# Attention seams: transposed keys and queries in banks of their own, the first head one slot ahead

## The chip, the cores and the metric

The kernel runs on one core of one Trainium2 chip. Its five engines are PE (TensorE, matmuls and transposes), DVE (VectorE), ACT (ScalarE), POOL (GpSimd) and SP (SyncE, which here only issues DMAs). PE writes into PSUM, which has eight banks of 128 partitions x 512 floats; DVE and ACT read them. The metric is the device time of one execution in microseconds (us), the median of several.

## The reference, cut to what matters

The input is `x` (4 x 512 x 512) with a context of the same shape, both float32. Two residual blocks follow each other:

```python
x = x + quantised_matmul(layernorm(x), ctx)          # both sides rounded to fp8 in blocks of 128
h = rmsnorm(layernorm(x), attn_norm_w)
q, k, v = h @ q_w.T, h @ k_w.T, h @ v_w.T            # 16 query heads, 4 key/value heads, 128 wide
q, k = rope(rmsnorm(q)), rope(rmsnorm(k))
attn = softmax(causal(q @ k.T / sqrt(128))) @ v      # four query heads share one key head
hidden = layernorm(x) + attn @ o_w.T
h2 = rmsnorm(hidden, ffn_norm_w)
out = x + hidden + sum over the top 2 of 8 experts of weight * down(silu(gate(h2)) * up(h2))
```

Queries, keys and values must be exact to float32 beyond what one pass of a matmul gives. So the kernel splits an operand into a high part (`_hi`, a copy rounded by ACT) and a low part (`_lo`, source minus high part, by DVE) and adds three products: high x high, high x low, low x high.

## The kernel before, in words

The program has a start, 16 iterations of attention (`for it in range(NIT)`) and the experts. An iteration `it = 4 b + g` is one batch `b` and one key head `g`. It has four heads `h`, and each head has four rows of 128 queries (`q = 0..3`), whose scores, maxima, exponentials and sums are made by PE (`score`, lines 696 to 705), DVE (`maxima`, L1264; `invert`, L1270 and, for the last row, the scaling L1275) and ACT (`exponentials`, L944). The probabilities of the head two heads back (`LAG = 2`) are turned by PE (`transpose_p`, L713), copied by ACT (`copy_p`, L950) and multiplied with the values (`values`, L724); the result is split by ACT (`hi_attn`, L958) and DVE (`lo_attn`, L1281).

Between these stand pieces of other work, put into slots by tables. A slot is `(head, place)` with place 1 to 3, and `units` yields for each slot, in this order, the pieces of the tables `FRONT_FIRST`, `ROUTE_FIRST`, `FILL`, `FRONT`, `ROUTE`, the weight splits and the experts' weights (`ew`). All engines walk the same slots, each doing its share, in the fixed order of its own program; semaphores tie the engines together. Place 1 of PE lies behind the scores of rows 0 and 1, place 2 behind row 2's score and ahead of the value products and row 3's score, place 3 at the end of the head. On ACT place 2 stands behind the copies of the probabilities and ahead of the last row's exponential. On DVE place 2 stands behind the last row's maximum and ahead of its reciprocal and scaling, place 3 behind `lo_attn`.

The pieces that matter here:

- `q`, `kv`: projections of the next iteration (`project`, L669), into banks 0 and 1; POOL ends them with a rope addition (L504).
- `o`: the output projection of the iteration before (`output`, L741), into banks 0 and 1 in turn, added to the hidden state by DVE (`add_output`, L1291). `m`: DVE scales the keys (`apply_norms`, L1258).
- `t` and `u`: the keys (piece 0) and the queries of heads 0 to 3 (pieces 1 to 4) are turned: four 128 x 128 transposes on PE (`transpose_qk`, L693), the high part by ACT (`hi_qk`, L963), the low part by DVE (`lo_qk`, L1286). Pieces 0 to 3 stand in the last slot (3,3), piece 4 (`u`) in the slot (0,1) of the next iteration. Their banks are `TR = (5, 6, 2, 5, 2)`. Piece 3 uses the bank of piece 0 and waits for its subtraction; piece 4 uses that of piece 2.
- `x..`, `y..`, `h..`: the next batch's first block, spread over the iterations g = 0 to 2. `xp` is its product with the context (L587, bank 2, added by DVE at L1140). `ht` turns the rows of the attention input (L613, bank 2; high part L869, low part L1166); the last of the four rows is in `FRONT_FIRST` at (3,3) of g = 2, ahead of piece 0.
- `rl`: the router's logits of the batch before (L647, bank 2, read by DVE at L1205), at g = 3; the last at (3,3).
- `ew`: in ten slots of an iteration from iteration 5 on, a piece of an expert's weights is split (L899 on ACT, L1193 or L1191 on DVE) and stored by DMA; ACT waits for the store before it reuses its buffer.

The first score of a head waits until the low part of its queries is there; before the first head's turned probabilities go to banks 5 and 6, PE waits for all of pieces 0 to 3:

```python
if i >= 2:
    need(pe, qk_lo, (G + 1) * j + {2: 0, 3: 1, 4: 3}[i])
...
pe.wait_ge(qk_lo, (G + 1) * it + h + 2)      # score, row 0 of head h
...
pe.wait_ge(qk_lo, (G + 1) * it + G)          # ahead of transpose_p
```

The end of an iteration together with the begin of the next is called a seam below; there are 15, numbered by the iteration that ends. At seams 2, 6 and 10 the slot (3,3) holds `ht` 3, at seams 7 and 11 `rl` 3, and at seams 1, 5 and 9 the slot (3,2) holds `xp` 2.

Of the kernel before, what the change touches and what calls it, by code (L numbers as in the profile page):

```python
# [19 lines left out]
B, S, D = 4, 512, 512  # L20
P = 128
NT = B * S // P
TT = S // P
# [3 lines left out]
G = HQ // HKV  # L27
# [42 lines left out]
def build(nc, x, ctxT, w_attn, wqkvo, qn, kn, cos, sin, w_ffn, gate, wexp, ident_d, mask_d, dispf_d, disph_d, out):  # L70
    with ExitStack() as ctx:
# [13 lines left out]
        def load_expert(sp, e, down):  # L85
# [22 lines left out]
        (2, 2): (('kv', 3),),  # L108
        (2, 3): (('o', 0), ('n', 0), ('o', 1)),
        (3, 1): (('m', 0), ('o', 2)),  # L110
        (3, 2): (('o', 3),),
        (3, 3): (('t', 0), ('t', 1), ('t', 2), ('t', 3))}


FRONT = ({(0, 1): (('cm', 0), ('cs', 0)),
# [23 lines left out]
          (1, 2): (('yh', 0), ('yh', 1)),  # L139
          (2, 1): (('yr', 0), ('yh', 2), ('yh', 3), ('ht', 0)),  # L140
          (2, 3): (('ht', 1),),
          (3, 1): (('ht', 2),)},
         {})
FRONT_FIRST = ({}, {}, {(3, 3): [("ht", 3)]}, {})
ROUTE = {(0, 1): (('rs', 0), ('rs', 1)),
         (1, 1): (('rs', 2),),
         (1, 2): (('rs', 3), ('rn', 0), ('rt', 0)),
# [26 lines left out]
NRAW = len(RAW)  # L174
RING_A = 6
LAG = 2


def need(engine, sem, count):

    if count > 0:
        engine.wait_ge(sem, count)


def units(it, h, place):


    b, g = divmod(it, HKV)
    slot = (h, place)
    if b + 1 < B:  # L190
        yield from FRONT_FIRST[g].get(slot, ())
    if g == HKV - 1 and b:
        yield from ROUTE_FIRST.get(slot, ())
    for kind, i in FILL.get(slot, ()):
        if (kind != "o" or it) and (it + 1 < NIT or kind in "ou"):
            yield kind, i
    if b + 1 < B:
        yield from FRONT[g].get(slot, ())
    if g == HKV - 1 and b:
        yield from ROUTE.get(slot, ())  # L200
    if it + 2 < HKV:
        yield from SPLIT_Q.get(slot, ())
    if 1 <= it <= HKV:
        yield from SPLIT_O.get(slot, ())
    if it >= FIRST_E and slot in SPLIT_E:
        m = (it - FIRST_E) * len(SPLIT_E) + SPLIT_E.index(slot)
        if m < NPIECE:
            yield "ew", m


def mixer(nc, x, ctxT, w_attn, wqkvo, wexp, wx_dram, qn, kn, cos, sin, w_ffn, gate_d, ident_d, mask_d, ident, logits, wcolf, extra, last_acc,
# [3 lines left out]
    with ExitStack() as ctx:  # L215
# [28 lines left out]
        kT = [[sb(f"kT{i}_{n}", [P, S], F32R) for n in ("hi", "lo")] for i in range(2)]  # L244
        v = [sb(f"v{i}", [P, TT, HD]) for i in range(LAG + 1)]
        prob = [sb(f"prob{i}", [P, sum(KEYS)]) for i in range(LAG + 1)]
        pT = sb("pT", [P, sum(QS)])
# [26 lines left out]
        zero = tables_at[:, 7 * HD:7 * HD + H]  # L274
        bank = [ctx.enter_context(nc.psum_tensor(f"bank{i}", [P, S], F32)) for i in range(8)]
        AUX, SC, PT, PV = 2, 3, 5, 7
        TR = (PT, PT + 1, AUX, PT, AUX)
        FIRST_T, FIRST_P = (PT, PT + 1, AUX, PV), (0, 1, SC, SC + 1)

        const_in, table_in, table_step = sem("const_in"), sem("table_in"), sem("table_step")  # L280
# [8 lines left out]
        q_rotated, kv_rotated, rope_added, k_ready = sem("q_rotated"), sem("kv_rotated"), sem("rope_added"), sem("k_ready")  # L289
        qk_tr, qk_hi, qk_lo = sem("qk_tr"), sem("qk_hi"), sem("qk_lo")  # L290
# [3 lines left out]
        at_hi, at_lo, o_done, o_added = sem("at_hi"), sem("at_lo"), sem("o_done"), sem("o_added")  # L294
# [12 lines left out]
        cm_turned, cm_row, cm_spread, cm_back, first_added = (sem(n) for n in ("cm_turned", "cm_row", "cm_spread", "cm_back", "first_added"))  # L307
# [262 lines left out]
        def _(pe):  # L570
# [79 lines left out]
            def project(j, t, kv):  # L650
                b = j // HKV
                if j == 0:
                    pe.wait_ge(hlo_ready, t + 1)
                elif t == 0 and not kv:
                    pe.wait_ge(hlo_ready, TT * (b + 1))
                if t == 0 and j < HKV:
                    pe.wait_ge(wqkv_lo, QKV * j + (QKV if kv else KC))
                elif t == 0:
                    for i in range(2):
                        pe.wait_ge(wkv_in[i] if kv else wq_in[i], 16 * (j - HKV + 1))  # L660
                need(pe, kv_rotated if kv else q_rotated, TT * j + t if j else t - 1)
                if t == 0:
                    need(pe, o_added, TT * (j - 2))
                if j == 0 and not kv:
                    pe.wait_ge(x1_ready, TT)
                o = kv_bank(j, t)[:, 0:2 * HD] if kv else q_bank(j, t)[:, :]
                for k in range(KC):
                    for n, (a, c) in enumerate(SPLITS):
                        last = nc.tensor.matmul(o, hT[a][:, k, t * P:(t + 1) * P], wkv(j, c, k) if kv else wq(j, c, k),  # L669
                                                start=(k == 0 and n == 0), stop=(k == KC - 1 and n == 2))  # L670
                last.then_inc(projkv if kv else projq, 1)

            def transpose_qk(j, i):
                it = j - 1
                if i == 1 and j == 0:
                    pe.wait_ge(first_added, TT)
                if i == 0:
                    pe.wait_ge(k_ready, j + 1)
                    need(pe, pt_copied, 16 * it + 4 * (G - LAG))
                if i == 2 and j:  # L680

                    b, g = divmod(it, HKV)
                    if g == 1 and b + 1 < B:
                        pe.wait_ge(x1_ready, TT * (b + 1) + 3)
                    if g == 2 and b + 1 < B:
                        pe.wait_ge(hlo_ready, TT * (b + 2))
                    if g == HKV - 1 and b:
                        pe.wait_ge(lg_ready, TT * b)
                if i >= 2:
                    need(pe, qk_lo, (G + 1) * j + {2: 0, 3: 1, 4: 3}[i])  # L690
                at = G * HD if i == 0 else (i - 1) * HD
                for t in range(TT):
                    last = nc.tensor.transpose(bank[TR[i]][:, t * P:(t + 1) * P], r[:, t, at:at + HD], ident[:, :])  # L693
                last.then_inc(qk_tr, 1)
# [12 lines left out]
            def transpose_p(s, j):  # L707
# [4 lines left out]
                for q in range(j, TT):  # L712
                    last = nc.tensor.transpose(bank[PT + j % 2][:, (q - j) * P:(q - j + 1) * P],  # L713
                                               prob[s % (LAG + 1)][:, P_AT[q] + j * P:P_AT[q] + (j + 1) * P], ident[:, :])
                last.then_inc(pt_tr, 1)
# [37 lines left out]
                project(0, t, False)  # L753
            for t in range(TT):
                project(0, t, True)
            for i in range(G):
                transpose_qk(0, i)
            for it in range(NIT):
                b, g = divmod(it, HKV)
                work = {"q": lambda t: project(it + 1, t, False), "kv": lambda t: project(it + 1, t, True), "o": lambda t: output(it - 1, t),  # L760
                        "t": lambda i: transpose_qk(it + 1, i), "u": lambda i: transpose_qk(it, i),
                        "xt": lambda t: transposes_x(b + 1, t), "xp": lambda t: product_x(b + 1, t), "ht": lambda t: transposes_h(b + 1, t),
                        "rt": lambda t: transposes_r(b - 1, t), "rl": lambda t: route(b - 1, t)}

                def fill(h, place):
                    for kind, i in units(it, h, place):
                        if kind in work:
                            work[kind](i)

                for h in range(G):  # L770
                    s = G * it + h - LAG
                    score(it, h, 0)
                    score(it, h, 1)
                    fill(h, 1)
                    if h == 0 or s == 0:

                        pe.wait_ge(qk_lo, (G + 1) * it + G)
                    if s >= 0:
                        transpose_p(s, 0)
                        transpose_p(s, 1)  # L780
                    score(it, h, 2)
                    fill(h, 2)
                    if s >= 0:
                        values(s, 0)
                        transpose_p(s, 2)
                        values(s, 1)
                        transpose_p(s, 3)
                    score(it, h, 3)
                    if s >= 0:
                        values(s, 2)  # L790
                        values(s, 3)
                    fill(h, 3)
# [20 lines left out]
        def _(act):  # L813
# [144 lines left out]
                nc.scalar.activation(aT[0][:, s % RING_A, :], bank[PV][:, :], ACT.Copy).then_inc(at_hi, 1)  # L958

            def hi_qk(j, i):  # L960
                act.wait_ge(qk_tr, (G + 1) * j + i + 1)
                o = kT[j % 2][0][:, :] if i == 0 else qT[0][:, i - 1, :]
                nc.scalar.activation(o, bank[TR[i]][:, :], ACT.Copy).then_inc(qk_hi, 1)  # L963

# [34 lines left out]
                square_kv(0, t)  # L999
            hi_qkv(1, 4)  # L1000
            hi_qkv(1, 5)
            for i in range(G):
                hi_qk(0, i)
            for it in range(NIT):
                b, g = divmod(it, HKV)
# [44 lines left out]
        def _(dve):  # L1050
# [230 lines left out]
                nc.vector.tensor_tensor(aT[1][:, s % RING_A, :], bank[PV][:, :], aT[0][:, s % RING_A, :].bitcast(F32), ALU.subtract).then_inc(at_lo, 1)  # L1281

            def lo_qk(j, i):
                dve.wait_ge(qk_hi, (G + 1) * j + i + 1)
                hi, lo = (kT[j % 2][0][:, :], kT[j % 2][1][:, :]) if i == 0 else (qT[0][:, i - 1, :], qT[1][:, i - 1, :])
                nc.vector.tensor_tensor(lo, bank[TR[i]][:, :], hi.bitcast(F32), ALU.subtract).then_inc(qk_lo, 1)  # L1286

# [41 lines left out]
            start_norms(0)  # L1329
            first_norms()  # L1330
            apply_norms(0)
            for i in range(G):
                lo_qk(0, i)
            lo_qkv(1, 4)
            lo_qkv(1, 5)
            for it in range(NIT):
                b, g = divmod(it, HKV)
# [480 lines left out]
```

## Time and profile before

| | |
|---|---|
| median of 3 runs | 1451.32 us (1448.89 to 1455.89) |
| the profiled execution's own time | 1451.23 us |
| its span, first to last instruction | 1449.4 us |
| mean granted clock of PE | 0.956 |
| PE busy | 1267.0 us, 87% |
| DVE busy | 838.8 us, 58% |
| ACT busy | 718.3 us, 50% |
| POOL busy | 382.4 us, 26% |
| PE, projections L669, three groups | 504.2 us |
| PE, transposes L693 | 320 weight loads and matmuls |

How to read it: busy time is an average over parts with different limits. The iterations run from about 90 to 1100 us, the experts from there on. PE's clock has two levels, 2.4 GHz (granted 1.0) and 1.2 GHz (0.5); a view that gives a value between them covers some time at either. An idle time in brackets is the engine's idle time just before the row, and behind the arrow stands who ended it.

### The profile page before, as it was taken

The numbers are of one execution on the slowest core, as the hardware profiler recorded it, in microseconds if no ns is written. First come the engines' busy times: TensorE is split into PE (matmuls) and PEld (weight loads), VectorE is DVE, ScalarE is ACT, GpSimd is POOL, SyncE is SP. The second block draws the span as 40 slices with busy tenths as digits, with TensorE's granted clock in tenths as the row PEclk, the third lists the DMA queues.
The fourth block names the chain that finished last, engine by engine and source line by source line (L and its number), as shares of the span: only waits on it lengthen the run. The fifth ranks groups of instructions, "written<-read, shape, count | busy, mean of one in ns | idle before, by whom it ended". The sixth has DMA issues, their size and how long they took to land. (4 is left out here: it accounts for less than half of the span.)

```text
span 1449.4 us, 22834 instructions
## 1 busy us (share of the span) xinstructions
PE 1267.0 (87%) x6845; PEld 1021.6 (70%) x6845; DVE 838.8 (58%) x2463; ACT 718.3 (50%) x2289; POOL 382.4 (26%) x545
## 2 busy tenths in 40 slices
PE   1767899999999989788999899998996389999995
PEld 0455776787776768677767777777775378889995
DVE  7667877666886666568767566555543322222321
ACT  6447756555675656465656646455543022223331
POOL 0213221232321223132213123232210123334332
PEclk9988999999999999999999999999998599999998
DMA  3270324350545465637545654754313797884443
GB/s 95 80 269 23 135 106 175 146 194 18 202 117 175 169 204 188 209 103 235 162 150 186 200 188 167 235 185 168 104 46 116 253 344 186 249 241 77 82 77 44
DMA packets 89734, 228.45 MB, mean 158 GB/s; under 512 B 12112, under 2 KB 49872, under 8 KB 79376
## 3 DMA queue, kind: packets, MB, share of 16 engines
q1 hardware_dynamic: 75840, 201.80, 39.7%
q0 software_dynamic: 10848, 24.71, 9.4%
q8 instruction: 60, 0.98, 0.3%
q10 hardware_dynamic: 2928, 0.49, 0.2%
q14 instruction: 58, 0.48, 0.1%
HBM read 146.71 MB, written 80.24 MB: 157 GB/s over the span
## 5 line engine op out<-in xcount | busy, mean ns | idle before, releaser
L527 POOL TENSOR_TENSOR prob<-prob,rtotal 128x128 f32<-128x128 f32 (+2 forms) x192 | 116.6, 613 | 457.5 <-DVE rtotal L1270 431.5
L1264 DVE TENSOR_SCALAR_CACHE_REDUCE prob<-bank,nscale 128x128 f32<-128x128 f32 (+3 forms) x256 | 135.0, 545 | 163.8 <-PE bank L705 163.5
L944 ACT ACTIVATE prob<-prob,bias 128x128 f32<-128x128 f32 (+3 forms) x256 | 144.8, 566 | 154.0 <-DVE prob L1264 153.3
L669 PE MATMUL bank<-w_hi,hT_hi 128*128 128x512 f32 x480 | 176.2, 367 | 14.6 <-DVE rot L1229 14.6
L724 PE MATMUL bank<-pT,v 128*128 128x512 f32 (+3 forms) x512 | 175.8, 445 | 8.8 <-ACT pT L950 8.1
L950 ACT ACTIVATE pT<-bank 128x512 f32<-128x512 f32 (+3 forms) x256 | 103.7, 433 | 138.2 <-PE bank L713 137.8
L669 PE MATMUL bank<-w_lo,hT_hi 128*128 128x512 f32 x480 | 164.0, 342 | 0.0
L669 PE MATMUL bank<-w_hi,hT_lo 128*128 128x512 f32 x480 | 164.0, 342 | 0.0
L1541 PE MATMUL gu<-we,xT_hi 128*128 x624 | 154.9, 331 | 3.3 <-DVE xT_lo L1657 2.7
L504 POOL TENSOR_TENSOR r<-r,rot 128x640 f32<-128x640 f32 x60 | 100.2, 1671 | 189.6 <-DVE rot L1229 189.6
L703 PE MATMUL bank<-kT_hi,qT_hi 128*128 128x128 f32 (+3 forms) x256 | 103.6, 405 | 14.6 <-DVE prob L1264 14.5
L713 PEld LDWEIGHTS bank<-ident,prob 128*128 128x128 f32 x640 | 82.7, 148 | 46.4 <-issue 34.1
L1541 PEld LDWEIGHTS gu<-we,xT_hi 128*128 128x128 f32 x624 | 108.2, 189 | 8.9 <-issue 6.6
L669 PEld LDWEIGHTS bank<-w_hi,hT_hi 128*128 128x128 f32 x480 | 93.3, 194 | 26.5 <-DVE rot L1229 18.1
L1517 POOL DMA_INDIRECT out<-y,ids x39 | 61.9, 1586 | 189.0 <-ACT y L1602 140.1
L713 PE MATMUL bank<-ident,prob 128*128 128x128 f32 x640 | 107.1, 284 | 0.0
L741 PE MATMUL bank<-w_hi,aT_hi 128*128 128x512 f32 x256 | 104.6, 409 | 2.7 <-issue 1.6
L1541 PE MATMUL gu<-we,xT_lo 128*128 x312 | 101.2, 324 | 0.0
L741 PE MATMUL bank<-w_hi,aT_lo 128*128 128x512 f32 x256 | 100.3, 392 | 0.0
L669 PEld LDWEIGHTS bank<-w_hi,hT_lo 128*128 128x128 f32 x480 | 92.2, 192 | 11.1
L741 PE MATMUL bank<-w_lo,aT_hi 128*128 128x512 f32 x256 | 100.0, 391 | 0.0
L724 PEld LDWEIGHTS bank<-pT,v 128*128 128x128 f32 x512 | 85.7, 192 | 20.2 <-ACT pT L950 8.2
(295 smaller groups left out, 2852.6 us busy)
## 6 DMA issues: line engine op xcount, KB each, us to landing
w_hi<-ws_scratch SPq DMA_DIRECT2D x24, 1024.0 KB, 5.1
w_lo<-ws_scratch SPq DMA_DIRECT2D x24, 1024.0 KB, 7.4
we<-wx_scratch SPq DMA_DIRECT2D x16, 1408.0 KB, 10.3
we<-wx_scratch SPq DMA_DIRECT2D x16, 768.0 KB
stage<-in_wexp SPq DMA_DIRECT2D x64, 176.0 KB, 2.4
wx_scratch<-ehi SPq DMA_DIRECT2D x64, 176.0 KB, 2.6
wx_scratch<-stage SPq DMA_DIRECT2D x64, 176.0 KB, 2.6
stage<-in_wqkvo SPq DMA_DIRECT2D x40, 256.0 KB, 3.3
```

What stands on the lines that cost most here:

```text
L504: nc.gpsimd.tensor_tensor(r[:, t, :], r[:, t, :], rot[t % 2][:, :], ALU.add).then_inc(rope_added, 1)
L527: nc.gpsimd.tensor_tensor(p, p, rtotal[:, 4 * h + q:4 * h + q + 1].broadcast_to([P, KEYS[q]]), ALU.mult).then_inc(prob_ready, 1)
L669: last = nc.tensor.matmul(o, hT[a][:, k, t * P:(t + 1) * P], wkv(j, c, k) if kv else wq(j, c, k), start=(k == 0 and n == 0), stop=(k == KC ...
L703: nc.tensor.matmul(o[:, 0:KEYS[q]], qT[a][:, h, q * P:(q + 1) * P], kT[it % 2][c][:, 0:KEYS[q]], start=(n == 0), stop=False)
L713: last = nc.tensor.transpose(bank[PT + j % 2][:, (q - j) * P:(q - j + 1) * P], prob[s % (LAG + 1)][:, P_AT[q] + j * P:P_AT[q] + (j + 1) * ...
L724: nc.tensor.matmul(bank[PV][:, j * P:S], v[it % (LAG + 1)][:, j, :], pT[:, PT_AT[j]:PT_AT[j] + QS[j]], start=(j == 0), stop=(j == TT - 1)) ...
L741: last = nc.tensor.matmul(bank[t % 2][:, :], aT[a][:, (G * o + h) % RING_A, t * P:(t + 1) * P], wo(c, h), start=(h == 0 and n == 0), stop= ...
L944: nc.scalar.activation(p, p, ACT.Exp, bias=bias[:, 4 * h + q:4 * h + q + 1], scale=-1.0, accum_out=total[:, 4 * h + q:4 * h + q + 1]).then ...
L950: nc.scalar.activation(pT[:, PT_AT[j]:PT_AT[j] + QS[j]], bank[PT + j % 2][:, 0:QS[j]], ACT.Copy).then_inc(pt_copied, 1)
L1264: nc.vector.tensor_scalar(prob[(G * it + h) % (LAG + 1)][:, P_AT[q]:P_AT[q] + KEYS[q]], bank[SC + q % 2][:, 0:KEYS[q]], nscale[it % 2][:, ...
L1517: pool.indirect_dma_start(out, bass.IndirectOffsetOnAxis(ap=ids[:, i:i + 1], axis=0), y[i % 3][:, :], None, compute_op=ALU.add).then_inc(y ...
L1541: last = nc.tensor.matmul(gu[i % 2][u][:, 0:I], xT[a][i % 2][:, k, :], we[:, bass.ds(at + (c * ECOLS + k * GU + u * I), I)], start=(k == 0 ...
```

## The change

Three things change. The four banks of the turned keys and queries are laid out anew: `TR = (5, 0, 6, 2, 2)` for piece 0 (keys) and pieces 1 to 4 (heads 0 to 3), so that pieces 0 to 3 have one each, and pieces 3 and 4 share bank 2. Piece 1 (head 0) goes first: it moves from (3,3) to (3,2), behind `o` 3, on PE, ACT and DVE alike, and the order of all five is `TURNS = (1, 0, 2, 3, 4)`, in the start too; all counts of the semaphores follow it. And the last turned rows of the attention input, `ht` 3, move from (3,3) to (3,2) of g = 2, behind head 0.

The waits follow the banks: piece 1 waits for the rope additions of the whole iteration and for the addition that read bank 0; the waits for bank 2 (`xp`, `ht`, `rl`) move from piece 2 to piece 3; piece 4 waits for pieces 0 to 3 where it waited for pieces 0 to 2; the turned probabilities wait for the pieces up to 2 where they waited for those up to 3, but they stand behind piece 4; the projection of an iteration waits until bank 0 was read.

```diff
-        (3, 2): (('o', 3),),
-        (3, 3): (('t', 0), ('t', 1), ('t', 2), ('t', 3))}
+        (3, 2): (('o', 3), ('t', 1)),
+        (3, 3): (('t', 0), ('t', 2), ('t', 3))}
...
-          (3, 1): (('ht', 2),)},
+          (3, 1): (('ht', 2),),
+          (3, 2): (('ht', 3),)},
          {})
-FRONT_FIRST = ({}, {}, {(3, 3): [("ht", 3)]}, {})
...
+TURNS = (1, 0, 2, 3, 4)
...
-        TR = (PT, PT + 1, AUX, PT, AUX)
+        TR = (PT, 0, PT + 1, AUX, AUX)
...
                 if t == 0:
                     need(pe, o_added, TT * (j - 2))
+                    need(pe, qk_lo, (G + 1) * (j - 1) + 1 if j else 0)
...
-                if i == 1 and j == 0:
-                    pe.wait_ge(first_added, TT)
+                if i == 1:
+                    pe.wait_ge(rope_added if j else first_added, TT * (j + 1))
+                    need(pe, o_added, TT * (j - 2) + 3 if j >= 2 else 0)
...
-                if i == 2 and j:
+                if i == 3 and j:
...
-                if i >= 2:
-                    need(pe, qk_lo, (G + 1) * j + {2: 0, 3: 1, 4: 3}[i])
+                if i == 4:
+                    pe.wait_ge(qk_lo, (G + 1) * j + G)
...
-            for i in range(G):
+            for i in TURNS[:G]:
                 transpose_qk(0, i)
...
-                        pe.wait_ge(qk_lo, (G + 1) * it + G)
+                        pe.wait_ge(qk_lo, (G + 1) * it + TURNS.index(2) + 1)
...
-                act.wait_ge(qk_tr, (G + 1) * j + i + 1)
+                act.wait_ge(qk_tr, (G + 1) * j + TURNS.index(i) + 1)
...
-                dve.wait_ge(qk_hi, (G + 1) * j + i + 1)
+                dve.wait_ge(qk_hi, (G + 1) * j + TURNS.index(i) + 1)
```

## Rows read from the trace of the kernel before

**Rows 1.** The page: busy time, share and instructions; PE's granted clock in 40 slices, tenths.

```profile
PE 1267.0 (87%) x6845; PEld 1021.6 (70%) x6845; DVE 838.8 (58%) x2463; ACT 718.3 (50%) x2289; POOL 382.4 (26%) x545
PEclk9988999999999999999999999999998599999998
```

**Rows 2.** Waits of PE: what waited for whom, us in total, times, longest.

```profile
PE bank L693 <- DVE kT_lo L1286: 25.7, 10, 5.7
...
PE bank L693 <- DVE hT_lo L1166: 10.6, 3, 4.9
```

**Rows 3.** Timeline of PE, seam 14: start, duration, instructions, [idle before, ended by].

```profile
1037.78 1.47 PE L693 MATMUL bank<-ident,r 128*128 128x128 f32 x12
1040.85 0.66 PE L693 MATMUL bank<-ident,r 128*128 128x128 f32 x4 [1.60 <-DVE kT_lo L1286]
1041.45 0.33 PE L703 MATMUL bank<-kT_hi,qT_hi 128*128 128x128 f32 x1
...
1042.38 0.61 PE L693 MATMUL bank<-ident,r 128*128 128x128 f32 x4
```

**Rows 4.** Timeline of DVE, seam 14.

```profile
1037.27 0.75 DVE L1264 TENSOR_SCALAR_CACHE_REDUCE prob<-bank,nscale 128x512 f32<-128x512 f32 x1 [3.33 <-PE bank L705]
...
1037.95 0.69 DVE L1291 TENSOR_TENSOR last_acc<-bank,last_acc 128x512 f32<-128x512 f32 x1
1038.91 0.16 DVE L1270 RECIPROCAL rtotal<-total 128x1 f32<-128x1 f32 x1 [0.28 <-ACT prob L944]
1039.11 0.49 DVE L1275 TENSOR_SCALAR prob<-prob,rtotal 128x512 f32<-128x512 f32 x1
1039.51 0.68 DVE L1281 TENSOR_TENSOR aT_lo<-bank,aT_hi 128x512 fp32r<-128x512 f32 x1
1040.11 0.68 DVE L1286 TENSOR_TENSOR kT_lo<-bank,kT_hi 128x512 fp32r<-128x512 f32 x1
1040.71 1.28 DVE L1286 TENSOR_TENSOR qT_lo<-bank,qT_hi 128x512 fp32r<-128x512 f32 x2
1042.18 0.69 DVE L1286 TENSOR_TENSOR qT_lo<-bank,qT_hi 128x512 fp32r<-128x512 f32 x1 [0.19 <-ACT qT_hi L963]
```

**Rows 5.** Timeline of ACT, seam 14: the last row's exponential.

```profile
1038.06 0.72 ACT L944 ACTIVATE prob<-prob,bias 128x512 f32<-128x512 f32 x1 [1.29 <-DVE prob L1264]
```

**Rows 6.** Windows: us, PE, PEld, DVE, ACT, POOL busy (instructions), PEclk, DMA share, GB/s.

```profile
339.00:344.00 5.00, 5.00 (x28) 4.57 (x28) 2.67 (x10) 2.94 (x8) 1.01 (x2) 0.66 0.00 0
...
1040.00:1045.00 5.00, 3.85 (x28) 3.20 (x29) 4.13 (x12) 3.25 (x10) 0.95 (x2) 1.00 0.96 322
```

**Rows 7.** Timeline of DVE, seam 5: the next batch's product is added.

```profile
464.91 0.68 DVE L1140 TENSOR_TENSOR acc<-bank,acc 128x512 f32<-128x512 f32 x1
```

**Rows 8.** Timeline of seam 6: PE's transposes, and ACT's wait for a store.

```profile
528.44 1.04 PE L693 MATMUL bank<-ident,r 128*128 128x128 f32 x8
534.33 1.84 PE L693 MATMUL bank<-ident,r 128*128 128x128 f32 x8 [4.86 <-DVE hT_lo L1166]
...
531.07 0.59 ACT L899 ACTIVATE ehi<-stage,wcolf 128x352 fp32r<-128x352 f32 x1 [4.06 <-DMA wx_scratch<-ehi]
```

**Rows 9.** Timeline of DVE, seam 7: the logits' read.

```profile
596.10 0.22 DVE L1205 TENSOR_SCALAR logits<-bank,extra 128x8 f32<-128x8 f32 x1
```

**Rows 10.** Timeline of ACT, seam 13: the wait for a store.

```profile
980.06 0.59 ACT L899 ACTIVATE ehi<-stage,wcolf 128x352 fp32r<-128x352 f32 x1 [4.89 <-DMA wx_scratch<-ehi]
```

**Rows 11.** Timeline of DVE, end of the start.

```profile
88.44 0.69 DVE L1286 TENSOR_TENSOR kT_lo<-bank,kT_hi 128x512 fp32r<-128x512 f32 x1 [1.82 <-ACT kT_hi L963]
89.22 0.69 DVE L1286 TENSOR_TENSOR qT_lo<-bank,qT_hi 128x512 fp32r<-128x512 f32 x1
...
91.58 1.66 DVE L1175 SCALAR_TENSOR_TENSOR w_lo<-stage,wcol,w_hi 128x256 fp32r<-128x256 f32 x4
```

**Rows 12.** Timeline of PE, seams 3 and 9.

```profile
338.81 0.66 PE L693 MATMUL bank<-ident,r 128*128 128x128 f32 x4 [1.60 <-DVE kT_lo L1286]
...
740.66 0.66 PE L693 MATMUL bank<-ident,r 128*128 128x128 f32 x4 [2.35 <-DVE kT_lo L1286]
```

More of the change, by code:

```diff
@@ L189, in units @@
     slot = (h, place)
-    if b + 1 < B:
-        yield from FRONT_FIRST[g].get(slot, ())
     if g == HKV - 1 and b:
@@ L1001, in _ @@
             hi_qkv(1, 5)
-            for i in range(G):
+            for i in TURNS[:G]:
                 hi_qk(0, i)
@@ L1331, in _ @@
             apply_norms(0)
-            for i in range(G):
+            for i in TURNS[:G]:
                 lo_qk(0, i)
```

## The prediction

> **What bounds the kernel now.** The page first: PE is busy for 87% of the span, and its granted clock is low only here and there [rows 1]. The span has three parts: a start of some 90 us, 16 iterations of attention up to 1100, experts after that. The diff touches only the start and the iterations, where PE has the most work. So next I read what PE waited for: the largest sums there end at line 693, the transposes of keys and queries, waiting for DVE's `kT_lo` (25.7 us in ten waits) and `hT_lo` (10.6 in three) [rows 2]. All lie at the seams between two iterations; there are 15. Then one seam on PE, DVE and ACT [rows 3 to 5]. The reader is to see a chain in which DVE hardly rests: score of the last row (ends about 1037.2) -> maximum at 1037.27 -> add of output 1037.95 -> reciprocal 1038.91 after 0.28 of idle -> scaling 1039.11 -> `aT_lo` 1039.51 -> `kT_lo` 1040.11 -> `qT_lo` of head 0 1040.71, and only then PE's first score of the next iteration at 1041.45. DVE operations of this size follow each other every 0.60 us (1039.51, 1040.11, 1040.71). PE has turned k, q0 and q1 by 1039.25 and is idle for 1.60.
>
> **What the change does to this seam (term A, five seams: 3, 4, 8, 12, 14, counted from 0).** Removed: the fourth transpose group's wait for `kT_lo`, since no bank is shared within the three groups left at (3,3). Moved: q0's four transposes, ACT's copy and DVE's subtraction go one slot earlier (no DMA is issued by the moved steps). Twelve transposes take 1.47 [rows 3], eight take 1.04 [rows 8], so four cost 0.43 of PE. No wait holds q0 there: its bank 0 was read by output 2's add, which in the trace ends before output 3's products do, and the same view shows the key's scaling (line 1258) done over 4 us before the maximum.
> But the slot lies before PE's last score of the iteration. PE has no idle time ahead of that score (DVE's maximum waited 3.33 for it [rows 4]), so the score, and all behind it, comes 0.43 later. And DVE's part of the slot stands behind that maximum, so `qT_lo` of head 0 does not leave the chain, it only moves forward in it. Seam 14 after: maximum 1037.70, add 1038.38, `qT_lo` 1038.98, reciprocal 1039.59 (its exponential, 0.80 behind the maximum [rows 5], is done by then), scaling 1039.79, `aT_lo` 1040.19, `kT_lo` 1040.79. A subtraction releases PE 0.74 after its start (1040.11 -> 1040.85, 1040.71 -> 1041.45), so the first score starts at 1041.53 against 1041.45: +0.08. What was saved is the 0.28 of DVE's idle time plus rounding; what was paid is 0.43. ACT is not late: its copy of q0 falls in the 1.29 it idled before the exponential.
> One wait grows. The fifth group (head 3, slot (0,1)) now shares bank 2 with head 2's q and waits for that subtraction, which before was due only behind it. After: `qT_lo` of heads 1 and 2 at 1041.39 and 1041.99, released 1042.73; the two scores take 0.93, so PE would be ready at 1042.46. It starts at 1042.73 against 1042.38: +0.34. Queued behind it are the seven transposes of the probabilities, hence ACT's copies and the value products. In exchange DVE's next maximum comes 0.2 earlier, which PE does not need. Where the clock is low the scores take longer and hide that wait (seam 3: +0.1); where DVE itself was late (seams 4 and 8) the 0.43 counts in part. By the same steps I get 0.1, 0.2, 0.2, 0.5 and 0.3: **+1.3 in five seams**. Bounds for one: -0.6 (q0 really off the chain) and +1.0 (0.43 of PE and 0.6 of DVE both in full).
>
> **Term B, seams 1, 5, 9.** Here the next batch's product is added in the same slot [rows 7]: DVE has no idle time between the add and the scaling, so head 0's 0.60 comes on top of PE's 0.43, minus the 0.60 taken from the end. First score +0.43; the fifth group +0.7 at full clock, +0.4 at seam 5: **+1.8**.
>
> **Term C, seams 2, 6, 10.** The last turned rows of the attention input move with q0: 0.86 of PE before the last score. In seams 6 and 10 ACT was held by a DMA (4.06 idle [rows 8]), and head 0's and these rows' copies and subtractions now run within it; the DMA was asked for a slot earlier and doesn't move. Once ACT is free, `hT_lo` is no longer in DVE's chain (0.60), the two last groups no longer start at 534.33 behind it at low clock (1.84), and the first score waits for `kT_lo` alone: about -1.5 and -1.6. In seam 2 nothing hides: both subtractions stay in the chain: +0.8. **-2.3**.
>
> **Term D, seams 7 and 11.** The group in bank 2 waits for the logits' read [rows 9]. It was head 1's, now it is head 2's, the last that the fifth group needs. With 0.43 and 0.60 ahead of it the read starts at 597.1, transposes 597.4, copy 598.0, subtraction 598.6, released 599.35 against 598.50: **+0.9 each, +1.8**.
>
> **Term E, seams 0 and 13, and the start.** DVE at 0 (busy with weights) and ACT at 13 (4.89 for a DMA [rows 10]) have the chain; head 0 hides in the wait, and the score needs `kT_lo` only: -0.6, -0.8. At the start head 0 is turned before k is ready, k alone stands ahead of the first score (released 0.74 behind 88.44, not behind 89.22), and DVE after subtractions at 88.44, 89.04, 89.64 is free at 90.24 rather than 91.58 [rows 11]: -1.3, which DVE's next work passes on; bound 0 if the weights' arrival rules. **-2.7**.
>
> Sum without the clock: 1.3 + 1.8 - 2.3 + 1.8 - 2.7 = **-0.1 us**.
>
> **Term F, the clock.** In 5 us behind each seam the granted clock was 1.00 at seven and 0.50 to 0.72 at eight [rows 6]; at 339 to 344 it was 0.66, so (1 - 0.66) x 5 = 1.7 us of full speed lost at the 1.2 GHz level. What came before: idle stretches of 2.8 and more, all five low; of 1.6 to 2.4, three of eight; of 0.9, neither of two. An idle of 1.60 stood before the low clock at seam 3 [rows 12] and before the full one at seam 14 [rows 3]. After, the third subtraction group no longer cuts the idle time: from the end of the three groups (1039.68) to 1041.53 it is 1.85 instead of 1.60, seams 1, 5, 9 gain some 0.6 in two pieces, 7 and 11 reach 1.4, 6 and 10 fall to 2 to 2.7. At the same frequencies I count nine or ten low seams instead of eight: one more, **+1.7**, bounds -3 and +5 falls (-5 to +8.5).
> The Trainium skill, TensorE: Matmul & The Clock Gate, section "A second HAM failure mode: psum-queue depth-cycling", says that short idles between groups of matmuls while banks are cycled make the clock swing between its levels. The rows of the seams agree, and by that rule this change, which packs the groups and leaves one unbroken idle, makes it worse: it is the second rival below.
>
> Forecast: the profiled run's own 1451.2 (span 1449.4 and 1.8 around it) + 1.6 = **1452.8 us**; the median of the runs, 1451.32, stands 0.1 from the profiled one, so no correction.
>
> **The rivals.**
> First, faster: q0 leaves the chain and PE's 0.43 is not felt, because something other than PE's own row of work holds the last score. Then each seam gives 0.6, 15 x 0.6 = 9, and three falls of the clock fewer, 5: 1451 - 14 = 1437. For it: the wait for `kT_lo` is the largest of PE. Against: the 3.33 that DVE waited for the score, and its order. Chance 0.13.
> Second, slower by the clock: stretches of 1.8 to 2.4 bring the 1.2 GHz level at nearly every seam. Six more falls, 10 us: 1461. It decides from four or five more falls on. For it: longer unbroken idle at ten seams. Against: 2.35 at seam 9 stood before full clock [rows 12]. Chance 0.16.
> Third, the change doesn't do what it says for another reason: the fifth group's wait, or the logits' read, simply takes the place of the one removed in every seam, +0.9 x 13 = 12 less what terms C and E give back, 5: 1458. It lies within what I call the same, chance 0.10. My own case: 0.61.
>
> **How the numbers follow.** A change of 0.5%, 7.3 us, is about what a measurement of this kernel can tell from none: bounds 1444 and 1458.6. The first rival lies below, the second above; my own and the third lie between, apart from tails of 0.01 to 0.02 each way. So faster 0.14, same 0.69, slower 0.17. Range 1445 to 1460: my own case with three falls either way, the third rival, part of the second, and the runs' own scatter (1448.9 to 1455.9).
>
> **What would show it.** Right: in the last slots PE's last score 0.4 later than before against output 3's products; on DVE `qT_lo` between the output's add and the reciprocal; from the maximum to the seam's first score 3.8 instead of 4.18; PE's wait for `kT_lo` at line 693 gone and one of some 1.8 before line 703 in its place; a short wait of 0.3 to 0.9 before the fifth group. Seams 6 and 10 shorter by 1.5. Eight to eleven low-clock seams. Wrong: the maximum not later than before, DVE idle between `aT_lo` and `kT_lo`, fewer than six low seams, or a total below 1444.

## The result

The changed kernel takes **1457.12 us** in the median of 12 runs (1454.11 to 1462.24), the kernel before 1452.57 in 12 runs beside them (1448.30 to 1457.43). The ratio is 1.0036, with a 95% interval of 1.0019 to 1.0053: slower by 0.4%, inside the half per cent that I had called "no change" (the interval's upper end lies just outside it), and inside the range (1445 to 1460). It is a small loss, but one clear of the noise: 4.5 us where I had forecast 1.6. The profiled execution took 1461.39 us with a span of 1459.6, near the upper end of its runs. Its experts, from the last masking matmul on, took 4.7 us longer than those of before (369.9 against 365.1), though no line of them was touched; over the profiles of all kernels here that part varies from 363.6 to 369.9. So below I compare stretches of the trace, not spans.

**The seam after.** First the largest wait of PE in the changed kernel; the columns are as in [rows 2].

```profile
PE bank L704 <- DVE kT_lo L1287: 30.2, 13, 4.8
```

The wait for `kT_lo` did not go. It moved from the transposes (25.7 us in [rows 2]) to the first score (now L704), and is longer. The wait for `hT_lo` did fall, from 10.6 to 3.2. Seam 14 on DVE, to be laid beside [rows 4]:

```profile
1043.31 0.75 DVE L1265 TENSOR_SCALAR_CACHE_REDUCE prob<-bank,nscale 128x512 f32<-128x512 f32 x1 [3.77 <-PE bank L706]
...
1043.99 0.69 DVE L1292 TENSOR_TENSOR last_acc<-bank,last_acc 128x512 f32<-128x512 f32 x1
1044.59 0.68 DVE L1287 TENSOR_TENSOR qT_lo<-bank,qT_hi 128x512 fp32r<-128x512 f32 x1
1045.19 0.15 DVE L1271 RECIPROCAL rtotal<-total 128x1 f32<-128x1 f32 x1
...
1045.78 0.69 DVE L1282 TENSOR_TENSOR aT_lo<-bank,aT_hi 128x512 fp32r<-128x512 f32 x1
1046.38 0.68 DVE L1287 TENSOR_TENSOR kT_lo<-bank,kT_hi 128x512 fp32r<-128x512 f32 x1
```

The same seam on PE, beside [rows 3]:

```profile
1047.12 0.33 PE L704 MATMUL bank<-kT_hi,qT_hi 128*128 128x128 f32 x1 [1.83 <-DVE kT_lo L1287]
...
1048.32 0.65 PE L694 MATMUL bank<-ident,r 128*128 128x128 f32 x4
```

The reader is to see four things. DVE waited 3.77 for the last score instead of 3.33: the 0.44 of head 0's transposes. `qT_lo` of head 0 stands between the add and the reciprocal, which no longer waits. From the maximum (1043.31) to the first score (1047.12) it is 3.81, before it was 4.18, so 0.37 of the 0.44 came back. And the fifth group starts 1.20 behind the first score, not 0.93: it waits.

**All 15 seams.** A window is laid around each seam, from the masking matmul of head 3's row 2 to that of head 0's row 2 in the next iteration. Columns: window; length, then busy times of PE, PEld, DVE, ACT, POOL (instructions), granted clock, DMA share, GB/s. Before, seams 4, 13, 14, and the sum of 15:

```profile
388.94:401.81 12.87, 11.10 (x67) 8.58 (x67) 11.14 (x41) 7.24 (x19) 3.50 (x5) 1.00 0.70 229
...
969.96:988.83 18.87, 13.18 (x68) 10.95 (x68) 9.49 (x24) 8.10 (x21) 1.84 (x3) 0.82 0.48 148
...
1031.56:1044.28 12.72, 11.12 (x68) 8.59 (x67) 8.08 (x22) 6.16 (x17) 1.17 (x2) 1.00 0.68 229
sum 232.68, PE 193.09 PEld 148.73 DVE 158.43 ACT 127.25 POOL 31.52; mean PE 12.87 PEld 9.92 DVE 10.56 ACT 8.48 POOL 2.10
```

The changed kernel, the same seams:

```profile
393.01:407.51 14.50, 12.58 (x68) 10.09 (x67) 11.16 (x41) 8.34 (x21) 4.19 (x6) 0.88 0.74 222
...
979.41:994.40 14.99, 12.57 (x68) 10.05 (x68) 8.97 (x24) 8.22 (x21) 1.84 (x3) 0.89 0.59 178
...
1037.16:1050.10 12.94, 11.02 (x68) 8.65 (x67) 7.99 (x22) 6.47 (x18) 1.48 (x3) 1.00 0.69 229
sum 236.90, PE 196.35 PEld 152.71 DVE 156.93 ACT 132.72 POOL 35.30; mean PE 13.09 PEld 10.18 DVE 10.46 ACT 8.85 POOL 2.35
```

The seams together are 4.2 us longer, about what the medians differ by. In the full lists of 15, eight windows lie below full clock before, ten after. Time at the 1.2 GHz level (twice the missing share times the length, summed over the windows) is 35 us before and 43 after. At seam 4 the low level makes 14.50 of what is 12.94 at full clock in the test with the idle stretch filled, below: 1.56 for one fall, which holds 3.4 us at that level. Taken over all 15, some 3 of the 4.2 are the clock and 1 is the order of work.

But one seam hides more. Seam 13 alone became 3.9 shorter, because ACT waited 0.88 for its store instead of 4.89, and that wait differs from kernel to kernel (see term E). The other 14 seams are 8.1 us longer; there the time at the low level rose from 28 to 39 us, which by the same price is some 5, and some 3 are the order. So it is in part luck that the sum agrees with the medians. And each of these lists is one execution. That the clock is lower does hold over all of them: its mean is 0.950 over the 12 runs of the changed kernel, and 0.954 or 0.955 over those of the kernel before in each of the three batches below (chips 7, 14 and 5).

### The profile page after: what moved, and what is told of

It is laid out like the page before. It is cut to its first block and busy times, and to the rows that moved or that the text cites. A ratio compares the mean times of both kernels' runs of the same rounds, so it can differ in the third digit from the quotient of the medians.

```text
span 1459.6 us, 22855 instructions
## 1 busy us (share of the span) xinstructions
PE 1275.5 (87%) x6845; PEld 1028.6 (70%) x6845; DVE 837.6 (57%) x2463; ACT 718.2 (49%) x2289; POOL 382.2 (26%) x545
## 5 line engine op out<-in xcount | busy, mean ns | idle before, releaser
L669 PE MATMUL bank<-w_hi,hT_hi 128*128 128x512 f32 x480 | 175.8, 366 | 14.8 <-DVE rot L1230 14.7
L704 PE MATMUL bank<-kT_hi,qT_hi 128*128 128x128 f32 (+3 forms) x256 | 104.4, 408 | 43.0 <-DVE kT_lo L1287 30.2
L714 PEld LDWEIGHTS bank<-ident,prob 128*128 128x128 f32 x640 | 86.2, 152 | 44.9 <-issue 33.7
```

The source lines that it names most:

```text
L704: nc.tensor.matmul(o[:, 0:KEYS[q]], qT[a][:, h, q * P:(q + 1) * P], kT[it % 2][c][:, 0:KEYS[q]], start=(n == 0), stop=False)
```

## The experiments

Each is compared with the runs of the kernel before on the same chip (medians 1453.45, 1453.11 and 1452.10 in the three batches) and, seam by seam, with the changed kernel. The diffs are against the changed kernel if nothing else is said. The changed kernel itself was not run again in these batches, so "less than the changed kernel" compares medians of different batches; with intervals of some 2.5 us on either side, a difference below about 3.5 us tells nothing. "Low" is the 1.2 GHz level. Which seams are low is read from one execution of each kernel, so I also give the mean granted clock over all runs where it matters.

**e1, banks and order alone.**

```diff
-        (3, 2): (('o', 3), ('t', 1)),
-        (3, 3): (('t', 0), ('t', 2), ('t', 3))}
+        (3, 2): (('o', 3),),
+        (3, 3): (('t', 1), ('t', 0), ('t', 2), ('t', 3))}
...
-          (3, 2): (('ht', 3),)},
+FRONT_FIRST = ({}, {}, {(3, 3): [("ht", 3)]}, {})
...
```

> The changed kernel with only its banks and its order (head 0, keys, head 1, head 2, head 3): head 0 and the last turned rows of the attention input go back to the slot (3,3). Chain theory (the moved transposes of PE delay the last score by 0.43 us a seam, DVE's chain keeps its length, the fifth group waits for head 2): the maximum lies where it lay before, the first score of an iteration comes 4.2 us behind the maximum as before, and only the fifth group's wait is left (0.1 to 0.3 a seam at full clock); the start keeps its gain of 0.9. Total within 2 us of the kernel before, so 1450 to 1454, about 4 below the changed one. Clock theory (one unbroken idle stretch per seam in place of a broken one brings the lower level more often): the idle is unbroken here too, so it stays as slow as the changed kernel, 1455 to 1459, with ten or more low seams.

Measured: 1456.80 us, ratio 1.0018 (1.0000 to 1.0037). The total misses the chain theory's 1450 to 1454. By the seams its terms hold: seam 4, at full clock in both, is 13.04 against 12.87 before, +0.17 for the fifth group's wait, and seam 7 is 13.55 against 13.37. What I had left out is the clock: 41 us of the seams at the low level, ten seams, as many as in the changed kernel. Here the clock theory's number was the right one. How much of the change's loss lies in the banks and order alone stays open: the 12 runs spread over 11 us, their interval overlaps the changed kernel's, and the mean clock (0.952) lies between that of before and the changed one.

**e2, PE's share of head 0 behind the last score.**

```diff
-                        if kind in work:
+                        if kind in work and (kind, i) != ('t', 1):
...
                     score(it, h, 3)
+                    if h == G - 1 and it + 1 < NIT:
+                        transpose_qk(it + 1, 1)
```

> The changed kernel, but PE turns head 0 right behind the last score of the iteration instead of ahead of it; ACT and DVE keep their order. Chain theory: the maximum comes 0.43 earlier in all seams where PE set it (11 of 15), the copy of head 0 still fits into ACT's idle time ahead of the exponential, so the first score comes 3.8 behind the maximum and each such seam is 0.4 shorter than in the changed kernel: 5 us less, 1450 to 1453. If the position of PE's transposes costs nothing (rival: all of the loss is the clock or the experts), the time stays at 1455 to 1459. Seams 2, 6 and 10 keep the 0.43 of the turned rows.

Measured: 1453.00 us, ratio 1.0001 (0.9986 to 1.0016), 4.1 less than the changed kernel. DVE at seam 14:

```profile
1034.36 0.75 DVE L1267 TENSOR_SCALAR_CACHE_REDUCE prob<-bank,nscale 128x512 f32<-128x512 f32 x1 [3.33 <-PE bank L706]
```

The wait for the last score is 3.33 again, and the seam 12.49 instead of 12.94. The low level stayed as it was (43 us in the seams), so I read this gain as the order of PE's work. At the seams at full clock in both (1, 3 and 14) it is 0.44 or 0.45 each time, the price of four transposes ahead of the last score. Elsewhere single seams moved by more, with the clock: seam 5 is 1.8 shorter, seam 7 2.0 longer.

**e3, the attention result split behind the turned pieces.** ACT's program is changed in the same way.

```diff
                     invert(it, h, 3)
+                    if h == G - 1:
+                        fill(h, 3)
                     if s >= 0:
                         lo_attn(s)
-                    fill(h, 3)
+                    if h < G - 1:
+                        fill(h, 3)
```

> The changed kernel, but in the last slot of an iteration ACT and DVE split the attention result (L959, L1282) behind the turned keys and queries instead of ahead of them. No work is added or removed. Chain theory (DVE's order from the last maximum to the keys' low part sets the seam): one operation of 0.60 less in the chain, the first score 3.2 behind the maximum instead of 3.8, 0.5 to 0.6 less in each of 15 seams: 8 us less, 1447 to 1451. Rival (PE's waits there are set by ACT or by the fifth group alone): no change, 1455 to 1459. Clock theory: the idle stretch falls from 1.85 to 1.25, so the lower level should nearly vanish from seams 3, 4, 12 and 14, another 3 to 5 us.

Measured: 1448.67 us, ratio 0.9969 (0.9946 to 0.9991). PE at seam 14:

```profile
1042.59 0.33 PE L704 MATMUL bank<-kT_hi,qT_hi 128*128 128x128 f32 x1 [1.22 <-DVE kT_lo L1290]
```

The maximum stood at 1039.39, so it is 3.20 to the first score, and the seam 12.35. DVE's order between the last maximum and the keys' low part sets this seam. The side forecast held for seams 3, 4, 12 and 14, which are at full clock with the shorter idle stretch; of these 3 and 14 were so in the changed kernel too. But seams 1, 5 and 9 stay or turn low (36 us in all), so the clock gave less than I expected.

**e5, the idle stretch filled.**

```diff
                     fill(h, 3)
+                    if h == G - 1 and it + 1 < NIT:
+                        need(pe, o_added, TT * it)
+                        for k in range(14):
+                            nc.tensor.transpose(bank[1][:, 0:P], ident[:, :], ident[:, :])
```

> The changed kernel with 14 transposes of the identity into bank 1 at the end of the last slot, about 1.5 us of PE work that nobody reads, placed into the idle stretch of each seam (15 seams). Clock theory (idle stretches at the seams bring the 1.2 GHz level, and that costs 1 to 1.7 us each time): low levels at the seams fall from nine or ten to four or fewer, total 5 to 8 us less, 1449 to 1452, although PE has more work. Chain theory without a part for the clock: the added work is hidden in the wait, so the time stays within 1 us of the changed kernel, 1456 to 1458; where it isn't hidden (seams 7 and 11) it adds up to 1 us each.

Measured: 1449.49 us, ratio 0.9966 (0.9950 to 0.9983), 7.6 less than the changed kernel, with more work. Windows of seams 4, 7, 14 and the sum:

```profile
390.77:403.71 12.94, 12.55 (x81) 10.17 (x80) 11.14 (x41) 7.58 (x20) 3.84 (x6) 1.00 0.70 226
...
585.47:602.12 16.65, 15.34 (x94) 13.09 (x94) 9.45 (x26) 7.98 (x21) 1.36 (x3) 0.90 0.67 233
...
1025.55:1038.49 12.94, 12.55 (x81) 10.17 (x81) 7.98 (x22) 6.48 (x18) 1.49 (x3) 1.00 0.69 229
sum 229.19, PE 206.55 PEld 163.94 DVE 157.21 ACT 126.30 POOL 31.98; mean PE 13.77 PEld 10.93 DVE 10.48 ACT 8.42 POOL 2.13
```

At seam 14, at full clock already in the changed kernel, the 14 transposes cost nothing: 12.94 both times. The low level is left at three seams (0, 7, 11) of ten, and the seams are 7.7 us shorter, as much as the medians differ by. The mean clock over the 12 runs rose from 0.950 to 0.963. At seams 7 and 11 the filling is not hidden: there PE idles (1.3 us) ahead of the last group of transposes, and the filling stands behind it, in front of the score. They are 2.4 longer each (seam 7 is 14.28 in the changed kernel). Both also have 3.4 us at the low level, where the changed kernel had none, so the 2.4 is not the filling alone.

**e4, the same split behind, but in the kernel before** (the diff of e3, against the kernel before).

> The kernel before (nothing of the change), with only the attention result's split (L958, L1281) behind the turned keys and queries in the last slot. Chain theory: DVE's chain from the last maximum to the first score loses one operation of 0.60 here as well, from 4.18 to 3.6, so seams 0.5 to 0.6 shorter each, 8 us less than before, 1444 to 1447. If the earlier test gained only because of the changed kernel's new order, nothing happens here: 1452 to 1455.

Measured: 1450.65 us, ratio 0.9980 (0.9961 to 1.0000). The seams move as expected (seam 14 12.25 instead of 12.72; their sum 221.1 instead of 232.7 with five low instead of eight), the total by 2.5 us instead of 8, outside the expected range. The profiled execution was among the fastest (span 1439.5), and the 12 runs spread over 17 us; over all of them the mean clock is 0.955, hardly above before, so five low seams are not what the others had. The mechanism is there without the change; why the median shows so little of it stays open.

**e7, the fifth group in a bank of its own.**

```diff
-        TR = (PT, 0, PT + 1, AUX, AUX)
+        TR = (PT, 0, PT + 1, AUX, 1)
...
-                    need(pe, qk_lo, (G + 1) * (j - 1) + 1 if j else 0)
+                    need(pe, qk_lo, (G + 1) * j if j and kv else (G + 1) * (j - 1) + 1 if j else 0)
...
                 if i == 4:
-                    pe.wait_ge(qk_lo, (G + 1) * j + G)
+                    need(pe, o_added, TT * (j - 1))
+                    need(pe, kv_rotated, TT * (j + 1))
```

> The changed kernel with the fifth group (head 3) in bank 1 instead of bank 2, so it no longer waits for head 2's low part; the keys' and values' projection waits for it instead, several us later. Chain theory with the fifth group's wait as a term: PE goes on right behind the two scores, at full clock 0.2 to 0.3 less per seam, seam 14 from 12.93 to about 12.7, seams at the lower level unchanged: 2 to 3 us less than the changed kernel, 1454 to 1456. Rival (that wait only moves PE's idle time to the next wait, for DVE's maximum): no change in the seams, 1456 to 1458.

Measured: 1452.87 us, ratio 1.0002 (0.9982 to 1.0022), 4.2 less than the changed kernel, more than the 2 to 3 expected. Seam 3, at full clock in both, is 12.62 instead of 12.94: the fifth group's wait was worth 0.32 and its removal is not given back at the next wait. The time at the low level in the seams stayed the same (42 us), so this gain too is the order of work; that it is more than forecast lies within the noise.

**e8, the three repairs together** (the diffs of e2, e3 and e7).

> The changed kernel with three repairs together: PE turns head 0 behind the last score, the attention result is split behind the turned pieces, the fifth group has bank 1. If the terms add (0.43 + 0.6 + 0.2 in most seams): 14 to 17 us less than the changed kernel, 1440 to 1444, seam 14 at about 11.8. If only one bound is there and the repairs overlap: 1447 to 1450, like the attention split alone.

Measured: 1440.91 us in 8 runs, ratio 0.9916 (0.9888 to 0.9944), 16 less than the changed kernel. The terms add: seam 14 is 11.60, 1.34 less than in the changed kernel (0.44 + 0.59 + 0.3 one by one).

**e9, the three repairs and the idle stretch filled** (as e5, with 10 transposes).

> The three repairs and, in the seam's idle stretch, 10 transposes of the identity into bank 1 (1.1 us of PE work that nobody reads). Clock theory: the low levels at the seams nearly vanish, another 5 to 8 us less, 1434 to 1438. Without a part for the clock, or if the idle stretch of 1.2 us left no longer brings the lower level: the same as with the repairs alone, 1440 to 1444.

Measured: 1438.90 us in 6 runs, ratio 0.9896 (0.9869 to 0.9922). The low levels did vanish (two seams, 0 and 13, 5 us in all; e8 had six, 25 us), and the seams' sum fell from 215.1 to 209.6. The mean clock rose from 0.955 to 0.962. Of that 5.5 the median shows 2, 0.9 us short of the expected range, and the intervals of e8 and e9 overlap, so whether the filling gains anything on top of the repairs is not shown. This is the best version I ran, 1.0% below the kernel before.

**e11, reciprocal and scaling behind as well** (e8, and `invert(it, h, 3)` of head 3 behind `fill` on DVE).

> The kernel with the three repairs, and DVE's reciprocal and scaling of the last row (L1271, L1276) also behind the turned pieces in the last slot. Chain theory: 0.2 + 0.4 less ahead of the keys' low part, which then waits for ACT's copy of the keys (behind the exponential, 2.1 after the maximum), so the first score comes 2.85 behind the maximum instead of 3.2: 0.35 to 0.4 per seam, seam 14 at 11.2 to 11.3, 5 us less than with three repairs, 1434 to 1437. If PE or ACT bounds the seam by now: seam 14 stays at 11.6 and the time at 1440.

Measured: 1441.75 us, ratio 0.9928 (0.9903 to 0.9953): no gain over e8, and seam 14 is longer, 12.00. First PE, then DVE at seam 14:

```profile
1026.40 0.33 PE L705 MATMUL bank<-kT_hi,qT_hi 128*128 128x128 f32 x1 [0.64 <-DVE kT_lo L1293]
...
1029.05 0.44 PE L705 MATMUL bank<-kT_hi,qT_hi 128*128 128x384 f32 x1 [0.33 <-DVE prob L1271]
```

```profile
1023.39 0.75 DVE L1271 TENSOR_SCALAR_CACHE_REDUCE prob<-bank,nscale 128x512 f32<-128x512 f32 x1 [3.33 <-PE bank L707]
...
1025.65 0.69 DVE L1293 TENSOR_TENSOR kT_lo<-bank,kT_hi 128x512 fp32r<-128x512 f32 x1 [0.30 <-ACT kT_hi L967]
...
1028.65 0.34 DVE L1271 TENSOR_SCALAR_CACHE_REDUCE prob<-bank,nscale 128x128 f32<-128x128 f32 x1
```

The first score does come earlier, 3.01 behind the maximum, now held 0.30 by ACT's copy. But all that was put off stands in DVE's queue ahead of the next iteration's first maximum, 5.26 behind the last one (4.86 in e8), and PE waits for it one score later. I read this as DVE's whole work in the seam bounding it by now, not the order.

**e10, the kernel before with the split behind and the filling ahead of the fourth group.**

```diff
+                if i == 3 and j:
+                    need(pe, o_added, TT * it)
+                    for k in range(10):
+                        nc.tensor.transpose(bank[1][:, 0:P], ident[:, :], ident[:, :])
                 if i >= 2:
```

> The kernel before with the attention split behind the turned pieces, and 10 transposes of the identity into bank 1 ahead of the fourth group, 1.1 us of PE work that nobody reads in an idle stretch of 1.0. It tells what the change itself is worth once the chain is shortened and the clock is kept up. Clock theory: low levels at the seams fall from five to two or fewer, 3 to 5 us less than without the filling, 1443 to 1447; then the changed kernel with its repairs and the filling (1438.9) is better by 5 to 8 us through head 0's early turn alone. If the filling costs what it takes: 1451 to 1455.

Measured: 1451.49 us, ratio 1.0001 (0.9981 to 1.0021), where "the filling costs what it takes" had put it. The clock did rise, from a mean of 0.955 in e4 to 0.961 over the 12 runs; the low level fell from five seams to three (0, 6, 13). But no time came of it. At seams 2, 7 and 11 the filling is not hidden and costs 0.8 to 0.9 each, and seam 6 was 19.74 instead of 16.62, with 6.8 us at the low level instead of 3.4; seams 6 and 13 hold long waits for stores.

The comparison with e9 says what the rest is worth: with the attention result's split behind and ten transposes of filling in both (at different places), the changed kernel with its repairs is 12.6 us faster. That is far more than the 5 to 8 expected, but it is a package: head 0's early turn, its own bank, PE's share of it behind the last score, the fifth group in bank 1, and the attention input's last rows. No run separates the early turn from the banks. The expectation's "through head 0's early turn alone" is not shown.

**e6, the attention input's last rows back in (3,3).**

```diff
-          (3, 2): (('ht', 3),)},
+FRONT_FIRST = ({}, {}, {(3, 3): [("ht", 3)]}, {})
...
```

> The changed kernel with the last turned rows of the attention input back in the slot (3,3), ahead of the keys; head 0 stays early. Only seams 2, 6 and 10 can move. Chain theory: the last score comes 0.43 earlier at seam 2 and the rows' low part stays in DVE's chain, so seam 2 at full clock is 0.4 shorter; at seams 6 and 10, where a store holds ACT, the rows' copy and low part come out from behind it, and the first score is 0.6 later. Sum within 1 us of the changed kernel, 1455 to 1459. If the rows' move is what the change lives on, these three seams get 1 to 2 us longer each: 1460.

Measured: 1455.87 us, ratio 1.0039 (1.0017 to 1.0061), within 1.3 us of the changed kernel. Seam 6 is 0.6 longer, seam 10 the same (16.54), seam 2 1.6 shorter, but it was at the low clock in the changed kernel and at full clock here. That only these three seams can move did not hold: seams 1, 3 and 7 turned low, seam 13 met a longer wait for its store (2.99), and the profiled execution has twelve low seams and a sum of 240.4. So much do two nearly equal programs differ in one execution each. By the medians the second half of the change is worth next to nothing either way.

## Why the prediction was right

The verdict, the range and the chain that it described were right. The size was not: +1.6 forecast, +4.5 measured. The order of work came out dearer by term C and the clock dearer by term F, and a shorter wait for a store at seam 13, which I can't claim, gave 3.1 more back than forecast. That the sum stayed inside the half per cent is in part luck.

- **Term A.** Seam 14 was to be +0.08 at the first score and +0.34 at the fifth group, with 3.83 from the maximum to the first score. Measured, from the begin of the window: +0.07 and +0.34, 3.81, and +0.22 for the whole seam. e2, e3 and e7 show its three parts one by one: 0.44 for PE's transposes, 0.60 per DVE operation in the chain, 0.32 for the fifth group's wait. Seam 12, low in both, is +0.52 (0.5 forecast), and seam 8 +0.47 (0.2). Seams 3 and 4 went their own way with the clock: -1.25, now at full clock, and +1.63, now low.
- **Terms B and D.** Forecast +0.7, +0.4 and +0.9, +0.9 at seams 1, 5, 7, 11; measured +0.59, +0.47, +0.91, +0.88. Seam 9 was +0.7 by the forecast and is +2.0, 1.4 of it the clock (18.19 at full clock in e5).
- **Term C** was mis-sized. Forecast -1.5 and -1.6 at seams 6 and 10 and +0.8 at seam 2, -2.3 in all; measured -0.35, -0.35 and +2.11, so +1.4. Seam 2 has one fall of the clock in it; in e5, at full clock, it is +0.67, near the forecast. At seam 10 the way from row 2's score to the first score did shrink, by 1.3 us. But the low clock then met dense work. Behind the first score, seven transposes of the probabilities in the changed kernel:

```profile
815.06 1.70 PE L714 MATMUL bank<-ident,prob 128*128 128x128 f32 x7
```

  and the same seven in the kernel before, where the low level had mostly fallen on a wait:

```profile
807.99 0.93 PE L713 MATMUL bank<-ident,prob 128*128 128x128 f32 x7
```

  I had counted falls of the clock, not what they fall upon. Seam 6 has 5.9 us at the low level instead of 3.4. In e5, where both are at full clock, they are 15.28 and 15.07, against 17.66 and 16.89 before (with a fall in each), so I read the clock as what took the gain.
- **Term E.** Seam 13 gave back 3.9 instead of 0.8. ACT waited 0.88 for its store instead of 4.89. The same seam is 17.5 in e3 (a wait of 3.63) and 17.4 in e6 (2.99), but 14.7 in e2 (0.33) and 13.1 in e7 (0.90, and at full clock), so I put it down to the store's timing and not to the change; no run isolates it. Seam 0 is +0.2 and not -0.6. The start: from the keys' scaling (L1258) to the first score it took 4.13 us before, now 3.28 (87.20 to 90.48); the gain of 0.85 is there, two thirds of what I had put down. It does not show in the profiled run, because the scaling itself came 1.4 later there.
- **Term F** was the term that decided. I put one more fall of the clock, +1.7; it was two more seams and 7 us more at the low level, about 3 us, and without seam 13 about 5. The clock is lower in the mean of all runs too (0.950 against 0.954 or 0.955). e5 shows that keeping PE busy in the idle stretch brings 7.6 us in the changed kernel; the same means raised the mean clock by 0.013 there, by 0.007 in e9 and 0.006 in e10, and gained 2.0 and nothing in those.
- **The second rival** (six more falls, 1461) had the right mechanism and too large a price. The Trainium skill, TensorE: Matmul & The Clock Gate, section "A second HAM failure mode: psum-queue depth-cycling", describes short idles between groups of matmuls bringing the clock down. The runs agree in part: an idle stretch of 1.82 stood at seam 4 before the low level, and both are gone with the filling; but the same 1.82 stood at seam 3 before full clock.
- **The first rival** (0.6 saved in each seam) fell. The 3.77 of DVE's wait shows that the last score is set by PE's own row of work, and e2 that the 0.44 is given back when PE's part moves behind it.
- **The third rival** (a new wait takes the place of the old one in every seam, 1458) has the number nearest to the measured one, but not its mechanism: +0.9 was there at seams 7 and 11 alone, and the fifth group's wait cost 0.17 (e1, seam 4) to 0.32 (e7, seam 3).

## What to carry to other kernels

An operation leaves a chain only if it leaves the order of the engine that carries the chain. Moving it one slot ahead within DVE's order brought the first score 0.37 us nearer to the maximum, while its producer, put ahead of the chain's first link on the busiest engine, cost 0.44. Putting what nobody waits for soon behind what somebody waits for now saved 0.6 per seam at full clock. Harmless work for PE in idle stretches that come back every iteration raised its clock in all three kernels tried, but paid for certain in one only (7.6 us; 2.0, within the noise; nothing). So check by the total, and check that the work is hidden: where it was not, it cost 0.8 to 0.9 for ten transposes.

## What the runs showed of the hardware that was not expected

Seam 4 took 14.50 us with one fall of the clock and 12.94 at full clock, there even with the 14 transposes more. Unread transposes that keep PE busy through an idle stretch raised the mean granted clock over all runs: 0.950 to 0.963 (e5), 0.955 to 0.962 (e8 to e9) and 0.955 to 0.961 (e4 to e10). In e5 that brought 7.6 us net (1457.12 to 1449.49) though PE ran 210 instructions more. What a fall costs depends on what it meets: at seam 10 seven transposes took 1.70 us under it, and 0.93 in the kernel before, where it had mostly fallen on a wait. How long the idle is does not alone decide: 1.60 stood before the low level at seam 3 and before the full one at seam 14 in the kernel before, and 1.82 before the low level at seam 4 and the full one at seam 3 in the changed one.
